# A two-layer graph network on one core: a quarter of the opening's normalisation on GpSimd, a bias DMA ahead of slot 1's moments, and the turned weights ahead of the last normalisations

## What is computed

```python
h = relu(layernorm(x))                       # layer 0
x = x + (adj @ (h @ w0) + b0)
h = relu(layernorm(x))                       # layer 1: five gated steps
for _ in range(5):
    m = adj @ h                              # in_matrix and out_matrix are both adj
    av = concat([m, m])
    u3 = h @ u3_w.T + u3_b
    z = sigmoid(av @ w3_w.T + w3_b + u3)
    r = sigmoid(av @ w4_w.T + w4_b + u3)
    hv = tanh(av @ w5_w.T + w5_b + (r * h) @ u5_w.T + u5_b)
    h = (1 - z) * h + z * hv
x = x + h
```

## Time and profile before

| | |
|---|---|
| median of 3 runs | 1474.78 us (1474.74 to 1474.79) |
| profiled execution, its own time | 1475.47 us |
| its span | 1473.5 us |
| PE busy | 1445.2 us, 98% |
| DVE busy | 1232.7 us, 84% |
| ACT busy | 937.0 us, 64% |
| POOL busy | 209.2 us, 14% |

### The profile page before, as it was taken

How to read it: one execution, slowest core, us unless ns; L and a number is a source line. 1 busy time by engine, 2 the same in 40 slices (tenths; PEclk the granted TensorE clock), 3 DMA queues, 4 the chain that set the end, 5 groups by cost and what they waited for, 6 DMA issues and landing times.

```text
span 1473.5 us, 20135 instructions
## 1 busy us (share of the span) xinstructions
PE 1445.2 (98%) x7017; PEld 676.6 (46%) x7017; DVE 1232.7 (84%) x1718; ACT 937.0 (64%) x1448; POOL 209.2 (14%) x392
## 2 busy tenths in 40 slices
PE   5899999999999999999999999999999999999999
PEld 4553444444444444444444444444444444444444
DVE  7889788888788888888778978889778888887778
ACT  4556656667568565776566666676665865566654
POOL 3440003310230004040203000413021100000000
PEclk9999999999999999999999999999999999999999
DMA  5513424371533323554432343347164232243322
GB/s 190 58 29 57 99 53 82 58 94 33 77 82 58 79 58 61 125 73 72 58 58 57 62 97 65 73 96 87 40 80 86 44 62 54 55 89 65 68 55 86
DMA packets 333171, 105.83 MB, mean 72 GB/s; under 512 B 310416, under 2 KB 327696, under 8 KB 333072
## 3 DMA queue, kind: packets, MB, share of 16 engines
q1 hardware_dynamic: 315696, 95.56, 31.7%
q0 software_dynamic: 16512, 8.39, 5.7%
q10 hardware_dynamic: 864, 0.59, 0.1%
HBM read 13.24 MB, written 8.39 MB: 15 GB/s over the span
## 4 chain that ended last, share of the span: by engine, by line
PE 88%; DVE 5%; ACT 1%; issue 1%; DVEq 0%
PE ps_a L706 30%; PE ps_c L706 15%; PE ps_b L706 7%; PE ps_u L793 7%; PE ps_u L797 7%; PE ps_u L795 7%; PE ps_v L793 4%; PE ps_v L795 4%; PE ps_v L797 4%; DVE rh L1483 1%; DVE rh L1479 1%; DVE h_lo L1490 1%; DVE area L1458 1%; DVE nx_lo L1435 0%; DVE rh L1466 0%
## 5 line engine op out<-in xcount | busy, mean ns | idle before, releaser
L706 PE MATMUL ps_a<-t_hi,nx_hi 128*128 128x512 f16 x576 | 218.3, 379 | 1.2 <-ACT rh L1059 1.2
L706 PE MATMUL ps_a<-t_lo,nx_hi 128*128 128x512 f16 x576 | 218.3, 379 | 0.0
L706 PE MATMUL ps_a<-t_hi,nx_lo 128*128 128x512 f16 x576 | 218.3, 379 | 0.0
L1077 ACT ACTIVATE rh<-ps_v,bias,w_inv 128x512 f32<-128x512 f32 x160 | 123.8, 777 | 84.5 <-PE ps_v L797 84.5
L1073 ACT ACTIVATE m_hi<-rh 128x512 f16<-128x512 f32 x138 | 86.4, 628 | 111.8 <-DVE rh L1466 111.4
L1518 DVE TENSOR_TENSOR rh<-rh,area 128x512 f32<-128x512 f32 x160 | 109.6, 696 | 54.3 <-ACT rh L1082 50.7
L1059 ACT ACTIVATE rh<-ps_a 128x512 f32<-128x512 f32 x138 | 81.3, 589 | 108.9 <-PE ps_a L706 100.8
L1082 ACT ACTIVATE rh<-ps_u,bias,w_inv 128x512 f32<-128x512 f32 x160 | 120.0, 773 | 20.8 <-PE ps_u L797 19.2
L1090 ACT ACTIVATE area<-ps_u,bias,w_inv 128x512 f32<-128x512 f32 x160 | 121.9, 770 | 16.9 <-PE ps_u L797 16.9
L1479 DVE SCALAR_TENSOR_TENSOR rh<-rh,area 128x1024 f32<-128x1024 f32 x78 | 95.3, 1222 | 44.0 <-ACT rh L1077 43.6
L1522 DVE TENSOR_TENSOR rh_lo<-rh,rh_hi 128x512 f16<-128x512 f32 x160 | 109.7, 687 | 20.1 <-ACT rh_hi L1095 17.8
(11 more groups left out here) (246 smaller groups left out, 3162.9 us busy)
## 6 DMA issues: line engine op xcount, KB each, us to landing
xr<-b_rows POOLq DMA_DIRECT2D x6, 1024.0 KB, 14.0
xr<-in_x_dram SPq DMA_DIRECT2D x5, 1024.0 KB, 5.7
out_dram<-xr SPq DMA_DIRECT2D x5, 1024.0 KB, 4.2
area<-in_adj_dram SPq DMA_DIRECT2D x8, 512.0 KB, 7.6
nx_hi<-s SPq DMA_TRANSPOSE x128, 2.4
nx_lo<-s SPq DMA_TRANSPOSE x128, 2.5
area<-in_x_dram SPq DMA_DIRECT2D x2, 1024.0 KB, 5.5
area<-b_rows POOLq DMA_DIRECT2D x2, 1024.0 KB, 13.4
```

What stands on the lines that cost most here:

```text
L706: last = nc.tensor.matmul(o[:, :], a[:, PLACE[k], j, :], b[:, k, j, :], start=(opens and j == 0 and n == 0), stop=(j == HB - 1 and n == 2) ...
L1077: nc.scalar.activation(cand[:, q, :], V_BANK[q][:, :], ACT.Tanh, bias=bias[:, BV:BV + 1], scale=w_inv[:, CAND:CAND + 1]).then_inc(cand_rea ...
```

## The change

GpSimd gets a function `normalise_fourth`: once the moments of both batches of slot 0 are there, it writes quarter 3 of slot 0 into `ysc` (four multiply-adds of 128 x 128 and one maximum with zero over 128 x 512) and counts `y_ready`. ACT no longer does this quarter. ACT's quarter 2 stands ahead of unit 11 instead of behind it. The bias DMA of slot 0 stands ahead of slot 1's moments instead of behind them. On ACT, `round_turned_weights` and `round_m(g, 3)` stand between quarters 2 and 3 of slot 1 instead of behind both and their rounding; on DVE, `rest_turned_weights` and `rest_m(g, 3)` stand ahead of K_S3's sum.

```diff
--- before.py
+++ after.py
@@ -241,6 +241,7 @@
         n_hi_done = [sem(f"n_hi_done{layer}") for layer in range(2)]
         y_late_done = sem("y_late_done")
         y_late_op = sem("y_late_op")
+        y_fourth_op = sem("y_fourth_op")
 
         c_done = sem("c_done")
         m_lo_done = sem("m_lo_done")
@@ -648,10 +649,22 @@
                 nc.gpsimd.tensor_scalar(ysc[:, 2 * HB:4 * HB, :], ysc[:, 2 * HB:4 * HB, :], 0.0, None, ALU.max
                                         ).then_inc(y_late_done, 1)
 
+            def normalise_fourth():
+
+                pool.wait_ge(moment_op[0], MOMENT_OPS)
+                for b in range(3 * HB, 4 * HB):
+                    last = nc.gpsimd.tensor_scalar(ysc[:, b, :], xr[0][:, b, :], rstd[0][:, b:b + 1],
+                                                   shift[0][:, b:b + 1], ALU.mult, ALU.add)
+                last.then_inc(y_fourth_op, 1)
+                pool.wait_ge(y_fourth_op, 1)
+                nc.gpsimd.tensor_scalar(ysc[:, 3 * HB:4 * HB, :], ysc[:, 3 * HB:4 * HB, :], 0.0, None, ALU.max
+                                        ).then_inc(y_ready[0], 1)
+
             moments(pool, 0, 0, 0, slice(0, 1), first_moment_op, stats_first)
             moments(pool, 0, 0, 0, slice(1, 2))
+            normalise_fourth()
+            bias_x(0, 0)
             moments(pool, 0, 0, 1)
-            bias_x(0, 0)
             scale_weights()
             bias_x(0, 1)
             for slot in range(2):
@@ -1100,11 +1113,11 @@
                     normalise(0, 0, 0, range(2))
                     round_n(0, 0, 0, 0)
                     act.wait_ge(top_scaled, 1)
-                    for unit in range(3 * HB):
+                    for unit in range(3 * HB - 1):
                         round_unit(unit)
                     normalise(0, 0, 0, range(2, 3))
+                    round_unit(3 * HB - 1)
                     round_rows(K_S4)
-                    normalise(0, 0, 0, range(3, 4))
                     round_n(0, 0, 0, 1)
                     round_m(g, 0)
                     round_weights()
@@ -1114,10 +1127,11 @@
                     round_m(g, 2)
                     round_rows(K_S1)
                     round_rows(K_S2)
-                    normalise(0, 0, 1, range(2, 4))
+                    normalise(0, 0, 1, range(2, 3))
+                    round_turned_weights()
+                    round_m(g, 3)
+                    normalise(0, 0, 1, range(3, 4))
                     round_n(0, 0, 1, 1)
-                    round_m(g, 3)
-                    round_turned_weights()
                     act.wait_ge(bias_done, 1)
                 elif p == 0:
                     round_m(g, 0)
@@ -1598,10 +1612,10 @@
                     rest_m(g, 2)
                     rest_rows(K_S1)
                     rest_rows(K_S2)
+                    rest_turned_weights()
+                    rest_m(g, 3)
                     sum_rows(K_S3)
                     rest_n(0, 0, 1, 1)
-                    rest_m(g, 3)
-                    rest_turned_weights()
                     sum_rows(K_B1)
                 elif p == 0:
                     rest_m(g, 0)
```

## The result

| | before | after |
|---|---|---|
| median (12 runs each, alternating) | 1475.16 us | 1478.72 us (1477.98 to 1479.77) |
| ratio, with its 95% interval | | 1.0026 (1.0017 to 1.0034) |
| profiled execution, its own time | 1475.47 us | 1478.62 us |
| its span | 1473.5 us | 1476.8 us |

The change makes the kernel slower by 3.6 us, 0.26%. The forecast was 1.3 us slower, with 0.76 on a change within 0.2%; the rival (b) had +3.1 us and a chance of 0.17. One of the twelve executions of before took 1693.05 us, and a few in the later series took far longer than the rest as well; the ratios and their intervals leave these out.

What follows compares the result with a forecast made beforehand. PE, busy 98% of the span, was taken as the bound, so only its holes and low clock count. +0.3 us without clock loss plus 1.0 for the clock gave +1.3: 1474.78 becomes 1476.1 us, range 1472.0 to 1478.8.

Steps and rivals of the forecast that it cites:

- rival (b): Bias DMA holds GpSimd 2.27 us and PE stays at 1.2 GHz up to unit 23: +3.1 us, 1477.9; chance 0.17.
- a late shift: Slot 1's moments on GpSimd end with the shift at 47.4 us instead of 43.94, 3.5 us later.
- a hole ahead of unit 21: PE idles 4.3 us ahead of unit 21, whose bank is free only at 54.3, in place of 1.7 us.
- The first hole: PE's idle 1.70 us ahead of direct_product(0, 2) at 40.46, of which 1.67 us was to go.
- Without any delay of the shift: If slot 1's shift on GpSimd came no later, K_S3's transposes start at 68.8: 3.1 us gained at most, 1471.7.
- rival (c): bn_stats on DVE stops GpSimd's quarter: shift near 50.4, +3.0 us on top of +1.3, 1479.1; chance 0.04.
- The chain: From unit 23's start through ACT and DVE to K_S3's transposes: 15.6 us, against 14.05 on PE's own path.
- a wait for x1: PE waits 1.5 us for x1 ahead of K_S3's transposes, because DVE becomes late.
- the second hole: PE's idle 2.05 us ahead of the first layer_out(0, 0, q) matmul at 62.39, all of it to go.
- the slow stretch behind it: PE at granted clock 0.51 from 63.20 to 66.65, costing 1.72 us in before, to go entirely.
- I take 1.43: Time the bias DMA takes on GpSimd ahead of slot 1's moments: 1.43 us, from bounds of 1.43 to 2.27.
- The clock. I take 1.0.: Half speed on PE from 52.9 to 56.4, around unit 21's start, costs 1.0 us, from bounds of 0 to 1.9.

Runs made afterwards that it cites:

- all three together: After with the bias DMA back behind the moments, K_S2's sum waiting for slot 1's moments and K_B1's sum behind opening_moments, against before: 1471.50 us, ratio 0.9974.

## Why the prediction missed the time

**The mechanism held.** Later moments under K_S2's sum, a late shift, a hole ahead of unit 21, then a chain through DVE to K_S3: each is in the trace where it was put. The first hole is gone entirely. Without any delay of the shift the prediction gave a gain of 3.1 us; with the DMA put back the gain is 2.7. The quarter on GpSimd took 1.75 + 1.49 us (forecast 1.72 + 1.43), beside bn_stats, so rival (c) falls. The page of the Trainium skill cited there (SBUF — State Buffer, Who interferes with whom) holds in this trace: all of 31.61 to 33.10 lies inside bn_stats, and it took 1.49 us where 1.43 had been worked out from rows without a neighbour.

**The chain held.** From unit 23 to K_S3 it was 15.42 us, forecast 15.6, with a wait for x1 of 1.20 us against 1.5. It is 15.41 with the DMA put back, and 15.42 with the turned weights alone. With all three together PE doesn't wait for x1 and its own path is 66.75 - 52.70 = 14.05 us, as forecast. The removal of the second hole and of the slow stretch behind it was forecast in full and came in full.

**The step that failed first: "I take 1.43" for the DMA.** The starts of the next instructions do stand 1.45 us behind the DMA's, as in before. But none of the three ends before the DMA's record is over: the first ends 2.56 us (35.19 + 1.11 - 33.74) behind its start, the others 0.2 us apart behind that, and each lasts 1.1 us instead of 0.2. The fourth starts 3.01 us behind the DMA (36.75 - 33.74); it starts 0.69 us behind the first (33.92 - 33.23) with the DMA put back. So the price is 3.01 - 0.69 = 2.32 us, the length of the record, where 1.43 was taken; with half the blocks the same working gives 1.78 us (36.39 - 33.92 - 0.69) and the record is 1.75. In before this was hidden: the instruction at 45.70 lasted 2.37 us and ended with K_S2's sum (45.70 + 2.28), so the distance of 1.43 us was a distance between starts, and its end gave no figure for the DMA. That was a reason to take the upper bound, 2.27, which was right. The DMA also began 0.64 us behind the maximum, not 0.33: the wait for the maximum to be counted was left out. The shift ended at 48.34 where 47.4 less 0.3 was forecast: 1.25 us late; the prediction's own 48.3 for a DMA of 2.27 us, less 0.3, is within 0.35 us of it. Of the lay-out by DVE's sums nothing else was wrong: the experiment with K_S2's sum held shows that its stop is there. The forecast said of the Trainium skill's sentence on GpSimd computing descriptors (DMA: Bandwidth & Descriptors, SWDGE vs HWDGE vs iDMA) that the 1.43 us agree; so do the 2.32 us of these traces.

**The second: "The clock. I take 1.0."** The slow stretch ran nearly up to unit 23 and cost 1.9 us (4.15 - 2.24), as rival (b) had it. The matmuls in the hole remove it and give 1.83 us in the trace. The forecast placed the slow stretch by the one example in before (begins 2.85 us behind the stop, lasts 3.45 us); in after it begins some 2.7 us behind the stop and lasts 6.8. Its sentence that a hole twice as long will cost at least one such stretch doesn't hold in general either: behind the hole of 3.30 us in the experiment with K_B1's sum the clock is 1.00.

**Together.** From the shift to unit 21 were 7.1 us, forecast 6.95. With 1.25 + 0.15 + 0.91 unit 23 is 2.3 us later than forecast, and less 0.2 in the chain K_S3 is 2.1 us later. 1.3 + 2.1 = 3.4 us; the trace has 3.1 (3.4 with the 0.3 us of origin), and the median 3.6. The hole of 5.53 us and K_S3 at 75.0 lie beyond what the prediction gave as signs of being right, 3 to 5 us and 72 to 74. Both misses are one end of bounds that the prediction had written down, and rival (b) combined them. The chance of both together, 0.17, was low for two bounds of which one, the DMA's, had the record's length behind it. Whether a longer hole makes the clock's cost larger is not shown: the low clock cost 1.91, 2.07, 1.64 and 2.07 us behind holes of 5.53 (after), 5.54 (old order of the turned weights), 5.53 (half the DMA) and 3.35 us (K_S2's sum held).

**What is open.** Why the clock falls behind one hole and not behind another: a low clock came behind 2.05 us (before, 0.51) and 3.35 us, and none behind 2.04 us and 3.30 us. Nor does it fall at a fixed distance from PE's stop: in the four traces just named it fell 2.7, 3.1, 2.1 and 1.2 us behind it, and stayed low for 6.8 us each time, in before for 3.4. Single runs of before lie mostly near 1475.2, but 5 of 27 in one series between 1472.6 and 1473.3. This would fit executions without the slow stretch, but no profile of such a run was taken. The records of single runs speak for it: these five have a mean granted clock of 0.998, and so do the four more in the other two series that took 1472.79 to 1473.00 us, while no other run of before in these series has that value. The trace with the DMA put back has 0.998 too, from 6.8 us at half speed between 10 and 30 us and no other in the opening; with the slow stretch of before on top it would be 0.9965, and before's runs at 0.996 and 0.997 took 1474.46 us and more.

The late K_B1's sum gained 0.9 us in the medians with GpSimd's quarter (1472.39 to 1471.54, two series) and nothing without it; up to the wait behind K_B1's transposes the traces have 0.6 us for both. Between runs of one mean granted clock the gain without the quarter is 0.5 to 0.8 us, so much of this contrast is the mix of executions; the groups are too small for more, and the mix may stand behind other differences of medians below 1 us in this part too.

## What to carry to other kernels

When an instruction that issues a transfer is moved on an in-order engine, take its whole record as its price, and what it has to wait for besides, not the distance between starts; if the instruction behind is held by something else, its end says nothing of the transfer. Then ask what the delayed work will now overlap with: here 3.0 us on GpSimd became 5.1 us because the tail slid under a sum on DVE, and 6.3 us in the median once PE's clock fell in the hole. Edits that come together are worth taking apart: the two harmless ones gave 0.16% together, and the third cost 0.43%.

## What the runs showed of the hardware that was not expected

- A DMA issued from GpSimd (x += bias, 16 blocks of 128x128) holds the engine for its whole record, 2.28 us; three instructions of 0.2 us that start in that time end only behind it (0.3, 0.5 and 0.7 us), and the one after them starts 2.32 us later than it would without the DMA. Half the blocks: 1.75 us, and 1.78.
- With no DVE instruction in the way, two neighbouring instructions on GpSimd (35.19 and 35.39 above) are shown overlapping for 0.9 us: both are shown as started while the DMA's record still runs (to 36.02), and they end behind it at 36.30 and 36.49. A start in the profile is no proof that an instruction is being worked on.
- The granted clock fell about 2.7 us into an idle stretch of 5.53 us and came back 4.0 us after work resumed, but in other traces it fell 1.2 us and 3.1 us after PE's stop; filling the stretch with 22 matmuls kept it at 2.4 GHz and gave 1.5 us. But a stretch of 3.30 us left it alone, and one of 3.35 us was followed by a loss of 2.07. A hole's clock cost is a chance here, between 0 and 2.1 us, and both ends belong in the range.
- Two engines' relative places move between executions: with the same code up to there, `shift` of slot 0 on GpSimd started 0.10 us ahead of bn_stats on DVE in one trace and 0.26 us behind it in another, and this decided whether one small instruction was caught by a sum of 2.28 us.
